# Context rows of six batches fetched as 32-row blocks and turned on VectorE, with GpSimd making their low part

## The reference

```
xn = layernorm(x)
kv = concat(context, xn)                     # 256 keys per batch
q = xn @ Wq      (32 heads of 128)
k = kv @ Wk ; v = kv @ Wv   (4 groups of 128)
x = x + softmax(q k^T / sqrt(128)) v @ Wo
y = layernorm(x)
x = x + ((y * in_scale) @ sign(W)^T) * out_scale + bias     # scales from an 8-way softmax router
```

## Time and profile before

| | us |
|---|---|
| median of 3 runs (663.86 to 664.73) | 663.97 |
| the profiled execution | 664.52 |
| its span in the trace | 662.7 |
| TensorE busy | 650.5 (98%) |
| VectorE busy | 483.6 (73%) |
| ScalarE busy | 376.3 (57%) |
| GpSimd busy | 397.7 (60%) |

### The profile page before, as it was taken

One profiled execution on the slowest core, in us unless ns is written; L12 is line 12 of the kernel. 1 busy time (PEld: TensorE's weight loads), 2 busy tenths in 40 slices (PEclk: granted clock), 3 DMA queues, 4 the chain that ended last, 5 costly groups with the idle time before them and its releaser, 6 DMA issues.

```text
span 662.7 us, 11042 instructions
## 1 busy us (share of the span) xinstructions
PE 650.5 (98%) x3292; PEld 546.4 (82%) x3292; DVE 483.6 (73%) x915; ACT 376.3 (57%) x925; POOL 397.7 (60%) x315
## 2 busy tenths in 40 slices
PE   6999999999999999999999999999999999999996
PEld 4888888888888888888888888888888888878875
DVE  4653232568897889788878887888788788978866
ACT  3335242575576557555764675557556755676643
POOL 3226855287477547645854595457546759964686
PEclk9999999999999999999999999999999999999999
DMA  8574676467887888878878888887778788776612
GB/s 318 206 254 176 239 250 227 146 226 255 275 275 262 272 259 277 254 260 271 277 245 268 263 279 268 254 278 253 266 259 274 258 283 259 258 255 224 189 66 82
DMA packets 96476, 161.68 MB, mean 244 GB/s; under 512 B 9064, under 2 KB 49256, under 8 KB 95392
## 3 DMA queue, kind: packets, MB, share of 16 engines
q1 hardware_dynamic: 96416, 160.97, 73.5%
HBM read 108.38 MB, written 52.56 MB: 243 GB/s over the span
## 4 chain that ended last, share of the span: by engine, by line
PE 92%; DMA 2%; issue 1%; SPq 1%; DVE 1%; ACT 1%; POOL 0%; POOLq 0%; DVEq 0%; ACTq 0%
PE bank L1520 30%; PE bank L1699 24%; PE bank L1625 20%; PE bank L1664 12%; PE bank L1779 2%; DMA p_low<-p_park 1%; PE bank L1680 1%; PE bank L1736 1%; DMA raw_a<-in_L_xattn_Wv 1%; DMA r_all<-r_park 1%; PE bank L1529 1%; PE bank L1728 0%; SPq L429 0%; PE bank L1751 0%; PE bank L1684 0%
## 5 line engine op out<-in xcount | busy, mean ns | idle before, releaser
L627 POOL TENSOR_TENSOR p_low<-p_low,p_high 128x1024 fp32r<-128x1024 f32 x64 | 154.0, 2407 | 158.1 <-ACT p_high L769 158.0
L1699 PE MATMUL bank<-wo_pair,oT 128*128 128x512 f32 x720 | 175.8, 392 | 0.2 <-POOL wo_pair L663 0.2
L895 ACT ACTIVATE prob<-bank,nmax 128x256 f32<-128x256 f32 x256 | 119.2, 471 | 70.7 <-DVE nmax L1251 65.6
L1699 PEld LDWEIGHTS bank<-wo_pair,oT 128*128 128x128 f32 x720 | 131.1, 188 | 25.1 <-POOL wo_pair L663 0.6
L1520 PEld LDWEIGHTS bank<-kg,qT 128*128 128x128 f32 x768 | 107.8, 190 | 9.9 <-issue 0.2
L1251 DVE TENSOR_REDUCE nmax<-bank 128x2 f32<-128x512 f32 x128 | 87.2, 684 | 37.8 <-PE bank L1520 37.3
L1520 PE MATMUL bank<-kg,qT 128*128 128x256 f32 x768 | 111.2, 282 | 0.0
L1271 DVE STREAM_TRANSPOSE p_turned<-prob 128x512 f32<-128x512 f32 x128 | 90.1, 705 | 26.6 <-ACT prob L895 21.4
L769 ACT ACTIVATE oT<-bank 128x512 fp32r<-128x512 f32 x64 | 38.3, 598 | 111.8 <-DVE bank L1285 111.8
L1625 PE MATMUL bank<-xT,wq_ring 128*128 128x512 f32 x336 | 82.4, 391 | 0.0
L657 POOL TENSOR_TENSOR wq_ring<-raw_a,wq_ring 128x512 fp32r<-128x512 f32 x42 | 54.6, 1299 | 27.3 <-ACT wq_ring L769 27.3
(11 more groups left out here) (139 smaller groups left out, 934.8 us busy)
## 6 DMA issues: line engine op xcount, KB each, us to landing
p_park<-p_turned SPq DMA_DIRECT2D x64, 512.0 KB, 3.7
p_low<-p_park SPq DMA_DIRECT2D x64, 512.0 KB, 5.8
kg<-k_park SPq DMA_DIRECT2D x64, 256.0 KB, 3.0
vg<-v_park SPq DMA_DIRECT2D x64, 256.0 KB, 3.6
v_park<-v_stage SPq DMA_DIRECT2D x8, 1024.0 KB, 4.3
raw_a<-in_L_xattn_Wq SPq DMA_DIRECT2D x32, 256.0 KB, 5.3
raw_b<-in_L_xattn_Wo SPq DMA_DIRECT2D x32, 256.0 KB, 5.3
k_park<-k_stage SPq DMA_DIRECT2D x8, 1024.0 KB, 4.6
```

Source lines behind the costliest of these rows:

```text
L627: nc.gpsimd.tensor_tensor(part, part.bitcast(fp32), p_high[:, :].rearrange("p i c q -> p (i c q)"), ALU.subtract).then_inc(p_lo, 1)
L895: ins = nc.scalar.activation(prob[:, p, j], s_bank[p][:, j * KEYS:(j + 1) * KEYS], ACT.Exp, bias=nmax[:, p, j:j + 1], accum_out=esum[:, t ...
L1699: last = nc.tensor.matmul(wo_bank[:, :], oT[:, s, h, :], wo_pair[:, w, h, :], start=((s, w) == TERMS[0] and h == 0), stop=((s, w) == TERMS ...
```

## The change

For batches 2 to 7 the context is loaded by four DMAs instead of one. DMA i fills partitions 32i to 32i+31. Every 128-row, 512-column tile is cut into 32x32 blocks, and block (j, c, i) is put so that a transpose inside each 32x32 block, which VectorE does in one instruction, gives the full transpose. A contiguous run of the source is then 32 floats, 128 bytes, where it was a row of 2048 bytes. The turned tile of batch b is written over the raw tile of batch b-2. ScalarE makes the high part from that tile in SBUF instead of from PSUM, and GpSimd, not VectorE, makes the low part. TensorE no longer transposes these six tiles. Batches 0 and 1 stay as they were.

```diff
+    BY_TENSOR = 2
             def load_c(b):
-                sp.dma_start(craw[:, b, :], ctx[b]).then_inc(c_in[b], 16)
+                if b < BY_TENSOR:
+                    sp.dma_start(craw[:, b, :], ctx[b]).then_inc(c_in[b], 16)
+                    return
+                rows = ctx[b].rearrange("(j s) (c i r) -> i s c j r", s=32, i=QB, r=32)
+                for i in range(QB):
+                    sp.dma_start(craw[32 * i:32 * i + 32, b].rearrange("s (c j r) -> s c j r", c=HC, r=32),
+                                 rows[i]).then_inc(c_in[b], 16)
...
             pool.wait_ge(const_ready, 2)
+            def ct_low(b):
+                pool.wait_ge(ct_hi, b + 1)
+                part = cT[:, :, :, b * T:(b + 1) * T]
+                nc.gpsimd.tensor_tensor(part[:, LO], craw[:, b - BY_TENSOR].rearrange("p (c t) -> p c t", c=HC),
+                                        part[:, HI], ALU.subtract).then_inc(ct_rested, 1)
             for b in range(B):
                 make_rstd(b)
+                if b > BY_TENSOR:
+                    ct_low(b - 1)
+            ct_low(B - 1)
...
             pool.wait_ge(proj_ready, 2 * B)
-            pool.wait_ge(ct_ready, B)
+            pool.wait_ge(ct_turned, B - BY_TENSOR)
+            pool.wait_ge(ct_rested, B - BY_TENSOR)
...
             def ct_half(b):
-                act.wait_ge(ct_ready, b + 1)
-                copy(cT[:, HI, :, b * T:(b + 1) * T],
-                     t_bank[1][:, :].rearrange("p (c t) -> p c t", c=HC)).then_inc(ct_hi, 1)
+                if b < BY_TENSOR:
+                    act.wait_ge(ct_ready, b + 1)
+                    turned_rows = t_bank[1][:, :]
+                else:
+                    act.wait_ge(ct_turned, b - BY_TENSOR + 1)
+                    turned_rows = craw[:, b - BY_TENSOR]
+                copy(cT[:, HI, :, b * T:(b + 1) * T], turned_rows.rearrange("p (c t) -> p c t", c=HC)
+                     ).then_inc(ct_hi, 1)
...
+            def ct_turn(b):
+                dve.wait_ge(c_in[b], 16 * QB)
+                if b - BY_TENSOR < BY_TENSOR:
+                    dve.wait_ge(ct_ready, b - BY_TENSOR + 1)
+                else:
+                    dve.wait_ge(ct_turned, b - 2 * BY_TENSOR + 1)
+                nc.vector.transpose(craw[:, b - BY_TENSOR], craw[:, b]).then_inc(ct_turned, 1)
...
                     if b + 1 < B:
-                        (ct_rest, xt_rest)[kc](b + 1)
+                        (ct_rest if b + 1 < BY_TENSOR else ct_turn, xt_rest)[kc](b + 1)
...
                     else:
-                        pe.wait_ge(lo_sem, b + 1)
+                        if kc == 0 and b >= BY_TENSOR:
+                            pe.wait_ge(ct_rested, b - BY_TENSOR + 1)
+                        else:
+                            pe.wait_ge(lo_sem, b + 1)
...
-                    if b + 1 < B:
-                        (ct_transpose, xt_transpose)[kc](b + 1)
+                    if kc == 1 and b + 1 < B:
+                        xt_transpose(b + 1)
+                    elif b + 1 < BY_TENSOR:
+                        ct_transpose(b + 1)
```

More of the change, by code:

```diff
@@ L221, in xattn_ffn @@
             sem(n) for n in ("stats_ready", "mv_ready", "rstd_ready", "rstd_step", "y_ready"))
-        xt_ready, xt_hi, xt_lo, ct_ready, ct_hi, ct_lo = (
-            sem(n) for n in ("xt_ready", "xt_hi", "xt_lo", "ct_ready", "ct_hi", "ct_lo"))
+        xt_ready, xt_hi, xt_lo, ct_ready, ct_hi, ct_lo, ct_turned, ct_rested = (
+            sem(n) for n in ("xt_ready", "xt_hi", "xt_lo", "ct_ready", "ct_hi", "ct_lo", "ct_turned", "ct_rested"))
         proj_ready, proj_hi, proj_lo = sem("proj_ready"), sem("proj_hi"), sem("proj_lo")
```

## The result

| | median us | profiled execution | span | granted clock |
|---|---|---|---|---|
| before | 663.91 (663.16 to 664.73, 4 runs) | 664.52 | 662.7 | 0.999 |
| changed | 672.72 (671.58 to 673.67, 4 runs) | 673.67 | 671.9 | 0.992 |

Ratio 1.0132, 95% interval 1.0116 to 1.0148: 8.8 us slower.

What follows compares the result with a forecast made beforehand. TensorE, holding 92% of the chain, was taken to bound the kernel: 2.6 us saved and 4.0 us of new stalls give +1.4, so a median of 663.97 + 1.4 = 665.4 us; whole range 662.8 to 672.5.

Steps and rivals of the forecast that it cites:

- What is removed: Prologue: TensorE's context transposes of batches 2 to 7, 6 x 0.44 = 2.6 us saved, all on the chain.
- The chain over GpSimd: Prologue: GpSimd's low part, behind its small operations, delays TensorE by 1.35 us at every second batch; 4.0 us of stalls.
- The price of a small packet: Context block loads: 13.5 ns of DMA engine time for each 128-byte packet, +6.2 us for six tiles.
- The queue: SyncE's queue: 18 more DMAs at 0.52 us each, first store of V out at about 21.5 instead of 20.07.
- The late store: Prologue: first store of V lands at 29.6, delay swallowed; as rival, slow small reads give 670.2 to 691, chance 0.34.
- L - 28.5: Prologue: total change in us when the first store of V lands at L, from about 29.9 on; 3.1 at 31.6.
- a landing after 31: Prologue: first store of V landing after 31, named as a sign of being wrong; the forecast landing was 29.6.

Runs made afterwards that it cites:

- e4: The changed kernel with contexts 5 to 7, x 6 and 7, the gate rows and the bias queued behind the first stores of V: 665.15 us, ratio 1.0024.
- e5: e4 with GpSimd's order turned, `ct_low(b+1)` ahead of `make_rstd(b+2)` instead of behind it: 661.49 us, ratio 0.9964.
- e1: The changed kernel with every context tile loaded as plain rows by one DMA, element order not the reference's: 665.15 us, ratio 1.0023.
- e3: The kernel before with contexts 2 to 7 loaded by four DMAs each of 32 whole rows: 664.12 us, one run.
- e9: The kernel before with contexts 2 to 7 each loaded by one DMA of 2048 runs of 128 bytes, data not the tile's: 672.56 us, one run.

## Why the prediction was wrong, point by point

- **What is removed.** Right, a little less: 0.40 us a batch by the step of 6.03, against 0.44; 2.4 us in all.
- **The chain over GpSimd.** Right in mechanism and size: predicted 7.34 from the moment when TensorE could start, measured 7.28 (17.36 to 24.64), with stalls at every second batch and not in between. `ct_low` took 1.27 us for a predicted 1.30, the block transpose 0.70. GpSimd's timeline after shows the order that makes it:

```profile
23.18 0.19 POOL L569 TENSOR_TENSOR rstd<-rstd,nwt 128x1 f32<-128x1 f32 x1
23.32 1.27 POOL L577 TENSOR_TENSOR cT<-craw,cT 128x512 fp32r<-128x512 f32 x1
```

- **The price of a small packet.** Right: from 22 to 29 us,

```profile
DMA packets 4703, 1.07 MB, mean 153 GB/s; under 512 B 4447, under 2 KB 4447, under 8 KB 4703
...
q1 hardware_dynamic: 4703, 1.07, 75.4%
```

  75.4% x 16 x 7 us = 84.4 us; less 256 packets of 2 KB at 87 ns, that is 14.0 ns for each of the others, where 13.5 was taken. That 13.5 came from writes; that reads cost nearly the same was not known beforehand. By the prediction's own terms 14.0 puts the landing at 30.0 and the total at +1.5, so this is not what failed. The estimate that was worked out from the Trainium skill (DMA: Bandwidth & Descriptors, section "Why small descriptors are slow"), 8.2 ns, was too low.
- **The queue. This step failed.** "SyncE's queue issues 18 more DMAs at (11.79 - 3.53) / 16 = 0.52 us, so its first store of V goes out at about 21.5 instead of 20.07." It went out at 29.74, 8.2 later. The runs show 0.64 for a block DMA,

```profile
L348 SPq DMA_DIRECT2D craw<-in_ctx x24: 584/637/892, 4.5 to 27.6; - x24
```

  and 0.62 to 2.24 us for the load of x behind four of them. The 24 block DMAs took 16.6 us of the queue where 0.52 each gives 12.4, and the six loads of x 7.4 where it gives 3.1: each of the two is about half of the miss. I priced an issue by DMAs of 128 runs, and the landing by engines that the queue keeps busy without a gap, as it did before, when it had issued all loads by 12.2 and they ended at 20.05. With 512 short runs in a DMA the queue had no such lead.
- **The late store.** Right as a mechanism and as a rival: last in the queue, ScalarE in front of it, everything of batch 3 behind ScalarE. But its price was tied to packets of 14 ns and more, and the packets cost what I said. The landing was to be 29.6, 3.4 us behind the last load; it was 36.04, 6.3 us behind a store that itself went out only at 29.74. By the prediction's own L - 28.5 that is +7.5, which is what the prologue shows without the slow product. The prediction had named a landing after 31 as a sign that it was wrong.
- **The clock. Left out.** The remaining 2.6 us of the prologue's 10.1 are product 6 at 1.2 GHz. The rule L - 28.5 held no term for what TensorE does after a long wait; in the trace before the only wait above 0.8 us is that for the first context tile, 3.5 us at the start.

## What to carry to other kernels

Price a DMA with many short runs three times: on the engines, on the queue that issues it, and for what is queued behind it. A store whose landing frees a buffer belongs ahead of loads that are needed late, as e4 shows. When work moves to another engine, the place in that engine's order decides: one pair of lines swapped turned +1.6 us (e4) into -2.6 (e5), each against the kernel before. And a long wait of TensorE can cost more than its length: here the wait of 7.2 us was followed by a product at the lower clock, while none of the waits of 1.0 us was.

## What the runs showed of the hardware

- An issue on SyncE's queue took 0.43 us for a tile of 128 rows (e1), 0.42 for 32 of its rows (e3), 0.64 for 512 runs of 128 bytes on 32 partitions and 0.56 for 2048 such runs on 128 partitions (e9). An ordinary load of x behind them took up to 2.24 us to issue, and up to 4.74 in e9.
- Whole rows loaded by quarters of 32 partitions cost the DMA engines more. In e3 the stretch from 5 to 19 us has

```profile
DMA packets 2552, 4.37 MB, mean 312 GB/s; under 512 B 418, under 2 KB 418, under 8 KB 2552
...
q1 hardware_dynamic: 2552, 4.37, 105.3%
```

  105.3% x 224 us, less 418 small packets at 13.5 ns, over 2134 packets is 108 ns for 2 KB, against 87 with 128 partitions. The row mixes tiles loaded in both ways, so a quarter's packet is dearer still. The first store, issued at 20.07 as before, took 7.8 us to land where it was 4.2, and product 6 came 0.6 us late (7.01 us behind product 4, where it was 6.43).
